# Raw padded images, a reordered head, and pooled columns summed over the partitions on GpSimd

## The reference, cut to what matters

```python
def _L0_conv_ref(x, w_route, b_route, w_experts, bn_gamma, ...):
    pooled = jnp.mean(x, axis=(2, 3))
    routing = jax.nn.sigmoid(pooled @ w_route.T + b_route)      # (16, 4)
    y = conv(x, w_experts, 3x3, padding 1)                      # 4 experts
    out = einsum('beohw,be->bohw', y, routing)
    ...                                                         # batch norm factors
    return jax.nn.silu(out)

def _L1_conv_ref(x, W):
    return conv(x, jnp.sign(W), 3x3, padding 1)

# x: (16, 128, 32, 32) float32; _gn: group norm, 32 groups of 4 channels
x = x + _L0_conv_ref(_gn(x), ...)
x = x + _L1_conv_ref(_gn(x), L1_conv_W)
```

## Time and profile before

| | us |
|---|---|
| median of 3 runs | 273.15 (273.0 to 273.46) |
| the profiled execution, its own time | 273.31 |
| the span in its profile | 271.5 |
| TensorE busy | 264.0 (97%) |
| VectorE busy | 255.3 (94%) |
| ScalarE busy | 219.6 (81%) |
| GpSimd busy | 43.5 (16%) |

### The profile page before, as it was taken

How to read it: one execution, slowest core, us unless ns; L and a number is a source line. 1 busy time by engine, 2 the same in 40 slices (tenths; PEclk the granted TensorE clock), 3 DMA queues, 4 the chain that set the end, 5 groups by cost and what they waited for, 6 DMA issues and landing times.

```text
span 271.5 us, 4138 instructions
## 1 busy us (share of the span) xinstructions
PE 264.0 (97%) x1339; PEld 183.0 (67%) x1339; DVE 255.3 (94%) x466; ACT 219.6 (81%) x450; POOL 43.5 (16%) x63
## 2 busy tenths in 40 slices
PE   8899999999999999999999999999999999999993
PEld 8544856758485766859586675848576685858663
DVE  5899999999999999999999999999999999995985
ACT  2489988998979798897979799897979895735870
POOL 3011020312112021212112021211202121210110
PEclk9999999999999999999999999999999999999999
DMA  7998836453726545261735545271645536272507
GB/s 215 417 374 304 303 140 154 62 115 72 141 80 96 138 78 154 34 123 78 126 109 77 154 63 121 69 138 77 100 135 77 154 38 121 81 134 97 77 2 155
DMA packets 10245, 35.20 MB, mean 130 GB/s; under 512 B 1264, under 2 KB 1904, under 8 KB 10224
## 3 DMA queue, kind: packets, MB, share of 16 engines
q0 software_dynamic: 4176, 15.21, 33.3%
q1 hardware_dynamic: 5616, 19.34, 18.7%
q10 hardware_dynamic: 432, 0.39, 0.4%
HBM read 11.34 MB, written 16.25 MB: 102 GB/s over the span
## 4 chain that ended last, share of the span: by engine, by line
PE 87%; DVE 8%; ACT 2%; issue 1%; POOL 1%; DVEq 0%; POOLq 0%
PE pc L590 40%; PE pb L555 14%; PE pa L555 14%; PE pe_ L555 13%; DVE U L1163 3%; PE pd L484 2%; PE pd L545 1%; POOL rstd L441 1%; PE ps L524 1%; PE ps L528 1%; DVE e_rows L1194 0%; ACT xn L869 0%; DVE lo L1285 0%; DVE U L1153 0%; DVE even L1172 0%
## 5 line engine op out<-in xcount | busy, mean ns | idle before, releaser
L1163 DVE SCALAR_TENSOR_TENSOR U<-we,route,U 128x1152 f32<-128x1152 f32 x45 | 63.6, 1412 | 0.6
L590 PE MATMUL pc<-lo,ws 128*128 128x496 f16 (+3 forms) x270 | 62.0, 375 | 0.0
L590 PE MATMUL pc<-hi,ws 128*128 128x496 f16 (+3 forms) x270 | 59.8, 375 | 0.5 <-ACT hi L930 0.5
L590 PEld LDWEIGHTS pc<-hi,ws 128*128 128x128 f16 x270 | 26.4, 98 | 30.0 <-issue 0.9
L590 PEld LDWEIGHTS pc<-lo,ws 128*128 128x128 f16 x270 | 27.7, 106 | 26.3
L555 PE MATMUL pb<-V,UM 128*128 128x256 f32 (+1 forms) x180 | 40.6, 375 | 0.6 <-DVE UM L1183 0.6
L555 PE MATMUL pe_<-V,U 128*128 128x256 f32 (+1 forms) x180 | 40.6, 375 | 0.0
L555 PE MATMUL pa<-V,UM 128*128 128x256 f32 (+1 forms) x180 | 40.5, 374 | 0.0
L555 PEld LDWEIGHTS pb<-V,UM 128*128 128x128 f32 x180 | 34.0, 190 | 5.9 <-issue 1.1
L441 POOL TENSOR_TENSOR rstd<-ve,nhalf 128x2 f32<-128x2 f32 (+1 forms) x19 | 15.4, 811 | 139.6 <-ACT ve L845 116.1
L555 PEld LDWEIGHTS pe_<-V,U 128*128 128x128 f32 x180 | 34.1, 190 | 3.8
(11 more groups left out here) (165 smaller groups left out, 408.8 us busy)
## 6 DMA issues: line engine op xcount, KB each, us to landing
X<-x SPq DMA_DIRECT2D x15, 512.0 KB, 5.3
out<-X SPq DMA_DIRECT2D x15, 512.0 KB, 2.6
out<-ev POOLq DMA_DIRECT2D x15, 512.0 KB, 5.5
X<-y POOLq DMA_DIRECT2D x14, 512.0 KB, 4.5
we<-w_experts SPq DMA_DIRECT2D x2, 768.0 KB, 8.4
ws_raw<-w_sign SPq DMA_DIRECT2D x1, 576.0 KB, 10.8
we<-w_experts SPq DMA_DIRECT2D x1, 512.0 KB, 6.4
out<-X SPq DMA_DIRECT2D x1, 384.0 KB, 2.8
```

What stands on the lines that cost most here:

```text
L590: mm = mm_(rows[:, r0 - first // W:r1 - first // W, c0:c1], ws[:, tap * C:(tap + 1) * C], plane((hi, lo)[part], i)[:, r0 + ky - 1:r1 + ky ...
L1163: v.scalar_tensor_tensor(out=nine(U[i % RING]), in0=expert(e), scalar=route[:, i, e:e + 1], in1=nine(U[i % RING]), op0=ALU.mult, op1=ALU.a ...
```

## The change

Images 1 to 15 are no longer normalised before the transform. `X` gets two more rows per image (`[C, B, PH, W]`), `pads` writes the image's group mean into them, `centring` makes the two numbers that this takes (the mean, and six times it, which `transform_plus` adds to the one point whose weights don't sum to zero), and the factor 1/std goes into the routing numbers instead (`routing`, a third form with `rstd` as scale and bias). `normalise` and the per-image `bias(c, IN)` go, and so do two of the three `xn` buffers.

From image 3 on `route_logits` is replaced by `sum_pooled` on GpSimd, a `partition_all_reduce` of the 128 x 4 tile `pooled`, at the end of iteration t and so behind `residual(t)`; `routing(c)` and `mix(c)` move to the end of ScalarE's iteration. Images 1 and 2 keep the product with ones.

In the head, image 1's sums move from VectorE (`part_stats`, `aggregate`, `columns`) to ScalarE (`mean_in(1)`, `var_in(1)`), the small products of images 1 and 2 move forward in TensorE's order, `sign_weights` moves behind `mix(2)`, and `group_stats` of iteration 1 stands between the two plus points.

Left out below: declarations of the new tiles and semaphores, counts of `zeroed`, and lines in which `xn[...]` only loses its buffer number. `P1_SUM` is 6.

```diff
-        X = sb("X", [C, B * HW])
+        X = sb("X", [C, B, PH, W])
         we = sb("we", [C, K, K, E, C])
...
         even = sb("even", [C, 2, KCO])
-        xn = [sb(f"xn{p}", [C, PH, W]) for p in range(RING)]
+        xn = sb("xn", [C, PH, W])
         e_rows = sb("e_rows", [C, TILES, TROWS, W])
...
         def img(i):
-            return X[:, i * HW:(i + 1) * HW]
+            return X[:, i, 1:1 + H, :].rearrange("p h w -> p (h w)")
...
+            def sum_pooled(c):
+                pool.wait_ge(pooled_ready, c + 1)
+                g.partition_all_reduce(pooled_sum[:, c, :], pooled[:, c, :], channels=C, reduce_op=bass.bass_isa.ReduceOp.add) \
+                 .then_inc(pooled_sum_ready, 1)
+
             def add_output(i):
...
                     residual(t)
+                if t + LAG - 1 < B:
+                    sum_pooled(t + LAG - 1)
...
                     wait(pe, nbias_mid_ready, c - LAG)
-                    pe.wait_ge(nbias_in_ready, min(c, B))
+                    pe.wait_ge(nbias_in_ready, 1)
+                    pe.wait_ge(centre_ready, 2 * (min(c, B) - 1))
                     pe.wait_ge(dev_ready, min(c, B) - 1)
-                    pe.wait_ge(th_ready, min(c, B))
...
                     pe.wait_ge(spread_ready, columns_to(c))
+                    if c < LAG:
+                        pe.wait_ge(centre_ready, 2 * c)
                 data = first_spread_col[:] if c == 0 else spread(c, k)
...
-            def plus_points(t):
+            def plus_point(t, j):
                 r = rank(t)
+                k = (P1, P2)[j]
                 pe.wait_ge(v_ready, 5 * r + 4)
                 wait(pe, sums_ready, 2 * r)
-                for j, k in enumerate((P1, P2)):
-                    pe.wait_ge(kernel_ready, 4 * r + k + 1)
-                    mm = point(t, pa, j, k, UM[t % 2][:, k, :])
-                mm.then_inc(m_ready, 1)
+                pe.wait_ge(kernel_ready, 4 * r + k + 1)
+                mm = point(t, pa, j, k, UM[t % 2][:, k, :])
+                if j == 1:
+                    mm.then_inc(m_ready, 1)
...
             route_logits(1)
+            group_mean(2)
             direct_part(0, 2, 0, slice(1, 3))
-            direct_part(0, 2, 1, slice(0, 2))
-            group_mean(2)
-            direct_part(0, 2, 1, slice(2, 3))
-            direct_part(0, 3, 0, slice(0, 1))
+            direct_part(0, 2, 1, slice(0, 1))
             group_var(2)
-            direct_part(0, 3, 0, slice(1, 3))
+            direct_part(0, 2, 1, slice(1, 3))
+            direct_part(0, 3, 0, slice(0, 2))
+            route_logits(2)
+            direct_part(0, 3, 0, slice(2, 3))
             direct_part(0, 3, 1)
-            route_logits(2)
...
                         sign_half(t - 2, 1, 1, TAP_ORDER[-1:])
-                    plus_points(t)
+                    plus_point(t, 0)
                     if t == 1:
                         group_stats(c)
+                    plus_point(t, 1)
                     end_points(t)
...
                     sign_half(t - 1, 0, 1)
-                    if c < B:
-                        route_logits(c)
                     sign_half(t - 1, 1, 0)
...
-            def normalise(i):
-                if i - RING >= ND:
-                    act.wait_ge(v_ready, 5 * (rank(i - RING) + 1))
-                elif i - RING >= 0:
-                    act.wait_ge(direct_ready, 2 * (i - RING + 1))
-                normalise_rows(i, 0, H)
+            def centring(i):
+
+                if in_one(i):
+                    act.wait_ge(gvar_ready, i + 1)
+                else:
+                    act.wait_ge(gnm_ready, gnm_chain(i))
+                for n, factor in enumerate((1.0, P1_SUM)):
+                    activation(centre[:, i, n:n + 1], gnm(i, IN), ACT.Copy, scale=-factor).then_inc(centre_ready, 1)
+
+            def pads(i):
+                act.wait_ge(centre_ready, 2 * i)
+                activation(X[:, i, 0:PH:PH - 1, :], ones[:, 0:2 * W].rearrange("p (a w) -> p a w", a=2), ACT.Copy,
+                           scale=centre[:, i, 0:1]).then_inc(pads_ready, 1)
...
             def routing(i):
-                act.wait_ge(logits_ready, i + 1)
-                activation(th[:, i, :], logits(i), ACT.Tanh, scale=0.5).then_inc(th_ready, 1)
+                if i < LAG:
+                    act.wait_ge(logits_ready, i + 1)
+                else:
+                    act.wait_ge(pooled_sum_ready, i - LAG + 1)
+                activation(th[:, i, :], logits(i) if i < LAG else pooled_sum[:, i, :], ACT.Tanh, scale=0.5).then_inc(th_ready, 1)
                 act.wait_ge(th_ready, i + 1)
-                activation(route[:, i, :], th[:, i, :], ACT.Copy, bias=0.5, scale=0.5).then_inc(route_ready, 1)
+                if i < ND:
+                    activation(route[:, i, :], th[:, i, :], ACT.Copy, bias=0.5, scale=0.5).then_inc(route_ready, 1)
+                else:
+                    act.wait_ge(rstd_ready, i + 1)
+                    activation(route[:, i, :], th[:, i, :], ACT.Identity, bias=rstd[:, i, IN:IN + 1],
+                               scale=rstd[:, i, IN:IN + 1]).then_inc(route_ready, 1)
...
             mix_first_part(0, 1)
+            mean_in(1)
             mix_first_part(0, 2)
+            var_in(1)
+            mix_first_part(0, 3)
             deviations(1)
-            mix_first_part(0, 3)
+            centring(1)
+            pads(1)
             variance(1)
-            bias(1, IN)
+            mean_in(2)
             pooled_plane(1)
-            normalise(1)
+            var_in(2)
             routing(1)
             mix(1)
-            mean_in(2)
-            var_in(2)
             deviations(2)
-            sign_weights()
+            centring(2)
+            pads(2)
             variance(2)
             mean_in(3)
-            bias(2, IN)
             pooled_plane(2)
-            normalise(2)
             var_in(3)
+            routing(2)
+            mix(2)
+            sign_weights()
             silu(0)
             mean_mid(0)
-            routing(2)
-            mix(2)
             squares(LAG)
...
                 deviation(c)
+                if c < B:
+                    centring(c)
+                    pads(c)
                 bias(c, MID)
...
                 if c < B:
-                    bias(c, IN)
                     pooled_plane(c)
...
                     mean_mid(t)
-                if c < B:
-                    normalise(c)
                 if t > 1:
...
                     mean_in(c + 1)
-                if c < B:
-                    routing(c)
-                    mix(c)
                 if c + 1 < B:
...
                     add_variance(c + 1, IN)
+                if c < B:
+                    routing(c)
+                    mix(c)
             last_mean()
...
                 v.tensor_scalar(bn_direct[:], bn_full[:], 1.0 / ACT_SCALE, None, ALU.mult).then_inc(bn_ready, 1)
-                v.tensor_scalar(bn_tiles[:], bn_full[:], INVERSE_SCALE / ACT_SCALE, None, ALU.mult) \
+                v.tensor_scalar(bn_tiles[:], bn_full[:], 0.5 * INVERSE_SCALE / ACT_SCALE, None, ALU.mult) \
                  .then_inc(bn_ready, 1)
...
                     return
-                dve.wait_ge(xn_ready, i + 1)
-                v.scalar_tensor_tensor(out=flat3(e_rows[:]), in0=flat(xn[i % RING][:, 0:H, :]), scalar=-4.0,
-                                       in1=flat(xn[i % RING][:, 2:2 + H, :]), op0=ALU.mult, op1=ALU.add) \
+                dve.wait_ge(x_loaded[i], 16)
+                dve.wait_ge(pads_ready, rank(i) + 1)
+                v.scalar_tensor_tensor(out=flat3(e_rows[:]), in0=flat(X[:, i, 0:H, :]), scalar=-4.0,
+                                       in1=flat(X[:, i, 2:2 + H, :]), op0=ALU.mult, op1=ALU.add) \
                  .then_inc(e_ready, 1)
...
                     return
-                rows = lambda first: xn[i % RING][:, first:first + H, :].rearrange("p (t k) w -> p t (k w)", k=TROWS)
+                rows = lambda first: X[:, i, first:first + H, :].rearrange("p (t k) w -> p t (k w)", k=TROWS)
                 v.tensor_tensor(f_rows[:].rearrange("p t k w -> p t (k w)"), rows(2)[:, :, W:3 * W],
...
                 vi = V[i % 2]
-                v.tensor_tensor(vi[:, :, P1, :], e_rows[:, :, 2, :], e_rows[:, :, 1, :], ALU.add) \
-                 .then_inc(v_ready, 1)
+                v.scalar_tensor_tensor(out=vi[:, :, P1, :], in0=e_rows[:, :, 2, :], scalar=centre[:, i, 1:2],
+                                       in1=e_rows[:, :, 1, :], op0=ALU.add, op1=ALU.add).then_inc(v_ready, 1)
                 v.scalar_tensor_tensor(out=vi[:, :, P2, :], in0=f_rows[:, :, 0, :], scalar=2.0,
...
             top_rows()
-            dve.wait_ge(x_loaded[1], 16)
-            part_stats(1, 0)
             for part in range(2):
...
                     mix_part(part, x)
-            part_stats(1, 1)
-            aggregate(1)
-            columns(1)
+            bn_factor()
+            bn_scales()
+            bn_offset()
```

(56 more changed lines are left out.)

2 lines of the change are left out of this document (1 added, 1 removed).

## The result

| | us |
|---|---|
| before, median | 273.3 (273.0 to 273.72) |
| after, median | 361.0 (359.63 to 361.91) |
| ratio | 1.320, 95% interval 1.318 to 1.322 |
| span of the profiled execution, before and after | 271.5 and 358.9 |

The changed kernel is slower by 88 us. The forecast was 344.5 with a range of 307 to 402. The measured 361.0 lies inside the range, 16.5 above the forecast; the third rival, a fall of TensorE's clock, turned out to be part of what happened.

A forecast was written before the change was run, and what follows sets the result against it. TensorE was taken to bound the kernel before, GpSimd's loop after. 271.5 - 1.14 (head) - 1.56 (products with ones) + 74.1 (GpSimd loop) = 342.9; with 1.81 and less 0.16, 344.5 us; range 307 to 402.

The forecast's parts named there:

- the third rival: TensorE's clock falls to 1.2 GHz in the loop's waits, adding 3.9 us per image, 395 in all; chance 0.18.
- the one wait per image: In the loop TensorE sets the pace, so whatever makes it wait once per image costs thirteen times.
- The products with ones: On TensorE's path in the loop, images 3 to 15 lose 0.12 us each, 1.56 us saved.
- The head: Before the loop, 1.14 us saved as TensorE's waits on VectorE and ScalarE go.
- I let the three waits go: In the head, TensorE's waits of 0.29, 0.33 and 0.52 us were all taken to vanish.
- the ends given for this term: For the head's 1.14 us saving: nothing, or a loss of about the same if two added sums make ScalarE late.
- The sum on GpSimd by itself: Behind the residual on GpSimd, the sum takes 0.73 us, between 0.13 and 0.9, and delays nobody.
- The loop at the full clock: From sum to sum over ScalarE and GpSimd: period 21.08 us, 5.70 per image above 15.38, 74.1 over thirteen.
- L: Time GpSimd needs to load a routine, ahead of each sum and each next power: 7.1 us, range 5.2 to 9.3.
- two loads per image at the full clock: The likeliest case: GpSimd loads routines before each sum and each power, clock unchanged; 344.5 us, chance 0.62.
- No load or a hidden one: Rival: GpSimd keeps both routines or a change costs under 2.3 us, only savings stay; 270.4 us, chance 0.15.
- One load only: Rival: the routine stays on GpSimd once loaded, only the first sum's interval stretches by 5.7 us; 276.1, chance 0.05.

The follow-up runs named there:

- e3_no_sum: The changed kernel with a tensor-tensor product of the same tile in the sum's place on GpSimd; 271.32 us.
- e1_ones: The changed kernel with the product with ones on TensorE for all images and no sum on GpSimd; 273.12 us.
- e2_no_power: The changed kernel with its sum, but from image 3 on VectorE writes a constant in place of GpSimd's power; 286.22 us.
- e5_warm: The changed kernel with 64 small products on TensorE between minus points and group statistics of images 2 to 14; 338.85 us.
- e4_one_sum: The changed kernel with the sum on GpSimd for image 9 alone and products with ones on TensorE for the others; 279.76 us.
- e6_sum_first: The changed kernel with GpSimd's order turned to power, sum, residual, output; 286.18 us, ratio 1.043 to the kernel before.

## Why the prediction held, and where it failed

**What bounds the kernel.** TensorE's path and the one wait per image: right. e3_no_sum has stages of 15.37 us (reckoned 15.38).

**The products with ones.** Reckoned 1.56 us, measured 1.80 (e1_ones less e3_no_sum).

**The head.** Reckoned 1.14 us, measured 0.2 (e1_ones against the kernel before, not clear of the noise, and 43.98 against 44.19). The step that failed is "I let the three waits go": they went, but the group statistics that were moved between the plus points brought a wait of 0.72 us, in every run with this head. They need image 0's sums behind its SiLU, and so the end of the direct convolution. Counted from the start of that convolution, the second minus points come 33.56 us later in the kernel before and 32.93 in e1_ones, so 0.6 was gained there; the convolution's own start lies between 10.3 and 11.1 us in the profiled executions (e2_no_power's aside), which can hide such a gain; why it moves stays open. The result lies inside the ends given for this term.

**The sum on GpSimd by itself.** Reckoned 0.73 us and harmless: harmless by e2_no_power and e3_no_sum; its length in the changed kernel is 0.74 to 1.48, median 1.19, so the upper end of 0.9 was too low.

**The loop at the full clock.** Reckoned 21.08 us per stage and 344.5 in all; e5_warm, where the clock stays up, has 20.72 in the stage shown and 338.85. The loss per image, against e3_no_sum, is 5.2 in place of 5.70: by the reckoning's own terms the shorter L takes 1.1 off and the longer sum gives 0.5 back.

**The clock.** This is where the likeliest case failed: "two loads per image at the full clock" had 0.62 and the fall of the clock 0.18, and the clock fell. The mechanism was the one described: the plus products behind the wait slow down, VectorE's last rows come later than GpSimd's loop, and the SiLU waits for them (2.29 us at 83.34). Its size was reckoned at 3.9 us per image with all plus and end products at half speed; it is 1.7. The rows show why: in the thirteen images the plus products take 4.04 to 5.22 us and the end products are back at 2.70 to 2.94, so 1.3 to 2.8 us are added in place of 5.08. The clock had risen again by the end points: 0.50 over the plus products and 0.92 over the end products in the stage shown, and in the next 0.50 from 97.13 to 99.00, 0.69 to 101.31 and 1.00 behind it. The SiLU's waits, 1.8 us per image in the mean, agree with the 1.7. The Trainium skill's page "TensorE: Matmul & The Clock Gate" (Part 1), by which activity is what releases the halved clock, agrees with both traces: 0.85 to 0.92 per stage with the waits empty, 1.00 with products in them.

**The other side.** No load or a hidden one was given 0.15; e3_no_sum shows its time, 271.3 (reckoned 270.4), with the sum left out. One load only, given 0.05, is ruled out by the gaps at all thirteen images.

**The number.** The range held 361.0 because it was made wide enough for both of the cases that it took in. The likeliest case alone gives 344.5; it came near to its own case, 338.85, in part because an L that was too long made up for a sum that was too short.

## What to carry to other kernels

Before a new kind of instruction is given to an idle engine, ask what stands between two of its uses: here a 1 us sum and a 0.7 us power in turn cost 13 us of GpSimd per image, and GpSimd's share of busy time didn't show it. Where such a cost can't be removed, its place decides: with the sum ahead of the residual the kernel lost 12 us, behind it 88. And a wait in a TensorE-bound loop was paid a second time, as the clock fell with it; harmless products in the wait gave a quarter of the loss back.

## What the runs showed of the hardware that was not expected

- The routine set seems to outlive an execution: the kernel whose last instruction on GpSimd is a sum had 7.65 us of idle time ahead of its first iota; the changed kernel, e4_one_sum, e5_warm and e6_sum_first, which hold sums too but end with a power, had 0.29 us there, and the kernel before a step of 0.13 without any. No run tested this by itself.
- The two directions differ: 5.6 to 6.4 us ahead of the sum, 6.6 to 7.6 ahead of a tensor-tensor instruction.
- The sum of a 128x4 tile over the partitions has a record of 0.69 us each time where no change of set stands before it (e2_no_power, from the second sum on), of 0.74 to 1.48 in the changed kernel and of 0.44 to 1.59 in e6_sum_first; which part of these is work, the records don't tell.
- A product of 128x128 ones with a 128x4 tile on TensorE costs 0.14 us of the path in float32 and next to nothing in float16.
- With TensorE waits of 4.2 to 4.9 us the granted clock of a stage was 0.85 to 0.92, and behind the wait it was 0.50 for all or part of the twelve plus products. Stages with waits of up to 2.0 us were at 1.00, and one with 3.05 us at 0.92 (e6_sum_first).
